# A recommender tower on one core: first-layer products emptied instruction by instruction, with one-sample product matmuls for two of four tiles

## The reference

```python
e = jnp.stack([tbl_0[ids[:, 0]], ..., tbl_26[ids[:, 26]]], axis=1)   # (512, 27, 128)
dot = jnp.einsum('bnd,bmd->bnm', e, e)
z = dot.reshape(512, 27 * 27)[:, idx]        # the 351 pairs i < j
h = jnp.concatenate([z, dense_ctx], axis=1)  # (512, 367)
h = jnp.maximum(h @ W_top1 + b_top1, 0.0)    # 367 -> 512
h = jnp.maximum(h @ W_top2 + b_top2, 0.0)    # 512 -> 256
y = h @ W_top3                               # 256 -> 1
```

## Time and profile before

| | us |
|---|---|
| median of 3 runs (lowest to highest) | 113.99 (113.63 to 115.16) |
| the profiled execution, its own time | 113.77 |
| its span, first to last instruction | 111.9 |
| outside the span | 1.87 |
| mean granted TensorE clock | 0.985 of full speed |

### The profile page before, as it was taken

How to read it: one execution, slowest core, us unless ns; L and a number is a source line. 1 busy time by engine, 2 the same in 40 slices (tenths; PEclk the granted TensorE clock), 3 DMA queues, 4 the chain that set the end, 5 groups by cost and what they waited for, 6 DMA issues and landing times.

```text
span 111.9 us, 2572 instructions
## 1 busy us (share of the span) xinstructions
PE 99.9 (89%) x984; PEld 84.3 (75%) x984; DVE 83.6 (75%) x192; ACT 82.9 (74%) x199; POOL 61.8 (55%) x68
## 2 busy tenths in 40 slices
PE   0956999999999999999997974999999999979882
PEld 0413778878888878888775964999899999969782
DVE  5599699999999999999698079787879438960000
ACT  2568999969969999987906399499999869951230
POOL 0778677777777777777776777677770000000000
PEclk9999999999999999999999997699999999999999
DMA  2989999967944752111221132122220000000000
GB/s 40 330 316 394 342 360 341 391 212 231 270 144 107 236 179 66 48 50 47 70 51 48 47 72 54 47 53 64 57 48 23 9 0 9 0 0 0 6 0 1
DMA packets 6207, 13.33 MB, mean 119 GB/s; under 512 B 2081, under 2 KB 2849, under 8 KB 6066
## 3 DMA queue, kind: packets, MB, share of 16 engines
q1 hardware_dynamic: 3714, 8.62, 23.3%
q0 software_dynamic: 2048, 4.20, 13.6%
q10 hardware_dynamic: 432, 0.34, 1.1%
HBM read 13.15 MB, written 0.00 MB: 118 GB/s over the span
## 4 chain that ended last, share of the span: by engine, by line
PE 67%; DVE 13%; ACT 8%; DMA 6%; issue 2%; SPq 1%; DVEq 0%
PE ps L249 18%; PE ps L250 17%; DVE G L398 12%; PE ps L289 9%; PE ps L307 6%; DMA raw<-in_hot_rows 6%; PE ps L272 5%; ACT G L460 5%; PE ps L261 5%; PE ps L320 3%; PE ps L329 2%; PE ps L338 2%; DVE eT L417 1%; ACT hi L434 1%; SPq L183 1%
## 5 line engine op out<-in xcount | busy, mean ns | idle before, releaser
L224 POOL DMA_INDIRECT E<-in_tbl,ids_sb x64 | 61.5, 962 | 21.7 <-issue 19.2
L386 DVE TENSOR_TENSOR onehot<-idsb,ps 128x1024 fp32r<-128x1024 int16 (+1 forms) x36 | 39.2, 1123 | 2.2 <-DMA idsb<-in_ids_hot 1.2
L398 DVE COPY_PREDICATED G<-mask,ps 27x48 f32<-27x48 int32 (+1 forms) x128 | 27.1, 212 | 11.1 <-ACT G L460 9.0
L460 ACT COPY G<-ps 27x48 f32<-27x48 f32 (+1 forms) x128 | 25.2, 197 | 6.1 <-PE ps L289 4.3
L249 PE MATMUL ps<-onehot,hi 128*128 128x512 f32 x66 | 26.6, 403 | 1.2 <-DVE lo L376 1.2
L250 PE MATMUL ps<-onehot,lo 128*128 128x512 f32 x66 | 25.9, 392 | 0.0
L289 PE MATMUL ps<-eT 128*64 128x54 f32 x512 | 17.7, 234 | 3.1 <-DVE G L398 2.3
L289 PEld LDWEIGHTS ps<-eT 128*64 128x64 f32 x512 | 17.0, 148 | 4.1 <-issue 3.6
L249 PEld LDWEIGHTS ps<-onehot,hi 128*128 128x128 f32 x66 | 12.4, 188 | 5.7 <-DVE lo L376 2.8
L307 PE MATMUL ps<-G,w_sb 128*128 128x128 f32 (+1 forms) x128 | 15.2, 277 | 0.0
L444 ACT ACTIVATE onehot_a<-idsb,num 128x1024 fp32r<-128x1024 int16 (+1 forms) x12 | 13.0, 1080 | 2.6 <-PE ps L250 1.4
(11 more groups left out here) (27 smaller groups left out, 57.7 us busy)
## 6 DMA issues: line engine op xcount, KB each, us to landing
raw<-in_hot_rows SPq DMA_DIRECT2D x10, 512.0 KB, 5.9
idsb<-in_ids_hot SPq DMA_DIRECT2D x5, 256.0 KB, 7.7
E<-in_tbl,ids_sb POOLq DMA_INDIRECT x64, 2.8
w_sb<-in_w SPq DMA_DIRECT2D x1, 1024.0 KB, 7.4
w_sb<-in_w SPq DMA_DIRECT2D x1, 512.0 KB, 7.4
raw<-in_hot_rows ACTq DMA_DIRECT2D x1, 256.0 KB, 3.9
raw<-in_hot_rows SPq DMA_DIRECT2D x1, 256.0 KB, 4.1
idsb<-in_ids_hot SPq DMA_DIRECT2D x1, 128.0 KB, 3.6
```

What stands on the lines that cost most here:

```text
L224: pool.indirect_dma_start(out=E[:, t % ES, slot, :], out_offset=None, in_=tables[f], in_offset=bass.IndirectOffsetOnAxis(ap=ids_sb[:, t * ...
L386: dve.tensor_tensor(onehot[:, u % ONEHOTS, 0:n * B], idsb[:, k0:k0 + n, :].rearrange("p k s -> p (k s)"), ps[:, NUMBERS, c:c + 1].to_broad ...
L398: op = dve.copy_predicated(place(t, w, s, m, n), mask[32 * m:32 * m + F, m:m + 4 * (n - 1) + 1:4].unsqueeze(2).unsqueeze(3) .to_broadcast( ...
L460: op = act.copy(place(t, w, s, m, n), spread(t, w, s, HALF + m, n))
```

## The change

- **Packing.** 24 of 27 slots now stand in 12 blocks of a ring, and three slots (`OWN` to `OWN`+2) are copied again into the five slots that were zeroed (`again`: two VectorE copies within `eT`, 3 x 512 and 2 x 512 elements, at the end of the first stage). So 12 blocks of 30 rows, and three rows left over, hold all pairs; the dense features and the bias go into the free rows. `G` and the first-layer weights have 3 blocks in place of 4: 12 matmuls a tile in place of 16. The four memsets of `eT` are gone.
- **Emptying.** A window is emptied in 16 steps, quadrant by quadrant within each row group. ScalarE signals after every copy, VectorE follows one by one; ScalarE starts a quadrant's next copy when VectorE is done with the one before in that quadrant. After the 16, VectorE does four more predicated copies (32 rows) for the pairs left over.
- **Products.** `EACH = [2, 1, 1, 2]`: tiles 0 and 3 keep two windows of two-sample matmuls. Tiles 1 and 2 have one window each, of 128 matmuls of one sample (32 stationary, 27 moving columns), four column strips in turn; its pieces are twice as long. Eight windows become six.
- **Order.** New lists for the three engines. Tile 3 is transposed in four groups (6, 5, 3, 2). The first part of pair 0 has its ScalarE one-hots last (parts 6, 7). The third layer and the second layer of tile 2 move ahead of the last tile's first layer.
- **Loads.** The second table is loaded ahead of the second ids, half a table moves from SyncE's to ScalarE's queue, dense features come in three small DMAs that wait for the first half of pair 0, as the weights behind them do. GpSimd has no `HOLDS`.

```diff
-GG = [list(range(a, b)) for a, b in [(0, 6), (6, 11), (11, 16)]]
+GG = [[list(range(a, b)) for a, b in zip((0, *ends), ends)] for ends in [[6, 11, 16]] * (T - 1) + [[6, 11, 14, 16]]]
...
-BY_ACT = [(2, 3), (3, 4), (3, 4), (3, 4), (3, 4), (3, 4)]
+BY_ACT = [(6, 7), (3, 4), (3, 4), (3, 4), (3, 4), (3, 4)]
...
-                        what, value = HOLDS.get(t * NG + slot, (None, 0))
-                        if what == "half":
-                            pool.wait_ge(half_done, value)
...
-                for g in range(2 * GB):
-                    at = (g % GB) * 2 * F
-                    for h in range(2):
-                        c = t * P + 64 * h + 2 * (2 * GB * w + g)
-                        mm = pe.matmul(ps[64 * h:64 * h + 64, dots_bank(t, w) + g // GB, at:at + 2 * F],
-                                       eT[:, c:c + 2, :].rearrange("p s f -> p (s f)"), eT[:, c:c + 2, 0:F], start=True, stop=True)
+                for g in range(16):
+                    if EACH[t] == 2:
...
+                    else:
+
+                        for s in range(4):
+                            c = t * P + 64 * (s // 2) + 2 * (16 * w + g) + s % 2
+                            mm = pe.matmul(ps[32 * s:32 * s + 32, window_bank(t, 0) + w, g * F:(g + 1) * F],
+                                           eT[:, c, :], eT[:, c, 0:F], start=True, stop=True)
...
-                for s in range(s0, s0 + ns):
-                    dve.wait_ge(base_out, 4 * (2 * t + w) + s + 1)
-                    for m in range(4):
-                        n = 4 if m == 0 else 3
-                        op = dve.copy_predicated(
...
+                for q in range(s0, s0 + ns):
+                    m, s = divmod(q, 4)
+                    dve.wait_ge(base_step, at + q + 1)
+                    dve.copy_predicated(place(t, w, s, m, ROWS_USED, KT), chosen(t, m, ROWS_USED, m, 4, KT),
+                                        spread(t, w, s, ROWS_USED, m, 4, KT)).then_inc(merge_step, 1)
+                if s0 + ns == 16:
+                    for s in range(4):
+                        dve.wait_ge(merge_step, at + s + 1)
+                        dve.wait_ge(base_step, at + 13 + s)
+                        dve.copy_predicated(place(t, w, s, 0, 32, 2), chosen(t, 0, 32, BLOCKS, 1, 2),
+                                            spread(t, w, s, 32, OWN, 1, 2)).then_inc(dots_out, 1)
...
+                    if m:
+                        act.wait_ge(merge_step, at + q - 3)
+                    act.copy(place(t, w, s, m, ROWS_USED, KT),
+                             spread(t, w, s, ROWS_USED, BLOCKS + m, 4, KT)).then_inc(base_step, 1)
```

More of the change, by code:

```diff
@@ L25 @@
 SPLITS = 4
-GB = 8
-SLOTS = 32
 WARM = 2
+EACH = [2, 1, 1, 2]
+WINDOWS = [(t, w) for t in range(T) for w in range(EACH[t])]
 V = [125000, 1000, 12500, 12500, 1250, 12500, 12500, 12500, 1250, 12500, 12500, 12500, 1000,
@@ L95 @@
[L95 to L100, removed]
+    compare 0 0 4, low 0 0, low 0 1, compare 0 4 2, low 1 0, compare 1 0 2, low 2 0, compare 1 2 1, low 1 1,
@@ L423, in _ @@
             act.dma_start(num[:, :], numbers).then_inc(num_in, 16)
[L424 to L425 removed]
+            for h in range(2):
+                for k in PAIRS[0]:
+                    act.dma_start(raw[:, k, half_of(k, h)], hot_rows[:, k, half_of(k, h)]).then_inc(raw_in[k, h], 16)
             act.dma_start(ident[:, :], eye).then_inc(eye_in, 16)
@@ L506, in _, with pair @@
             act.copy(y[:, :], ps[:, L3, 0:T]).then_inc(y_out, 1)
[L509 to L527 removed]
+def first_layer_rows():
+    take = np.zeros((BLOCKS + 2, 32), np.int32)
+    rows = np.full((BLOCKS, 32), -1)
+    def pair(i, j):
+        a, b = sorted((ORDER[i], ORDER[j]))
+        return b * (b - 1) // 2 + a
+    for k in range(BLOCKS):
+        for i in range(ROWS_USED):
+            if i < OWN:
+                other, second = i % BLOCKS, i >= BLOCKS
+                take[k, i] = second if other <= k else not second
+                if i == k + BLOCKS:
+                    continue
+            else:
+                take[k, i] = i < F
+            slot = i if i < F else AGAIN[i - F]
+            if i == k:
+                take[k, i] = 0
+            rows[k, i] = pair(slot, k if take[k, i] else BLOCKS + k)
+    for n, i in ((0, 30), (0, 31), (1, 31)):
+        take[BLOCKS + n, i] = 1
+        rows[4 * n, i] = pair(AGAIN[i - F], OWN + n)
     assert sorted(rows[rows >= 0]) == list(range(F * (F - 1) // 2))
[L529 removed]
+    return take, rows
 def kernel(**inputs):
@@ L536 @@
     W1 = np.asarray(inputs["W_top1"])
-    rows = first_layer_rows()
+    take, rows = first_layer_rows()
     w1 = np.zeros((4, 32, KT, H1), W1.dtype)
-    for k in range(COLS):
-        used = rows[:, k] >= 0
-        w1[k % 4, used.nonzero()[0], k // 4] = W1[rows[used, k]]
-    w1[2, 0:DENSE, KT - 1] = W1[F * (F - 1) // 2:]
-    w1[2, DENSE, KT - 1] = np.asarray(inputs["b_top1"])
+    for k in range(BLOCKS):
+        used = rows[k] >= 0
+        w1[k % 4, used.nonzero()[0], k // 4] = W1[rows[k, used]]
+    rest = np.zeros((3 * 2 * KT, H1), W1.dtype)
+    rest[0:DENSE] = W1[F * (F - 1) // 2:]
+    rest[DENSE] = np.asarray(inputs["b_top1"])
+    w1[1:, ROWS_USED:] = rest.reshape(3, 2, KT, H1)
+    mask = np.zeros((4, 32, BLOCKS + 2), np.int32)
+    for m in range(4):
+        mask[m] = take.T
     ids = np.asarray(inputs["ids"]).reshape(2, 2, P // 4, T, F).transpose(0, 2, 1, 3, 4)
```

193 lines of the change are left out of this document (90 added, 103 removed).

## The result

The changed kernel takes **109.74 us** (median of 4 runs, 109.06 to 110.25), the kernel before beside it 114.57 (113.63 to 115.67): a ratio of 0.960, 95% interval 0.949 to 0.971. It is faster. I had forecast 112.9 in a range of 109.0 to 116.6. The time lies in the range, but it is that of my first rival (109.3), not of the case I had called likeliest.

What follows compares the result with a forecast made beforehand. First stage bound by TensorE and VectorE together, the second's middle by a mixture, its last tile by emptying. First product 61.8, last emptying 103.6, tail 5.6 to 109.2, plus 1.84 and 1.87: 112.9 us, range 109.0 to 116.6.

Steps and rivals of the forecast that it cites:

- first rival: One-sample products: strips run fully side by side at 0.029 us a matmul, time 109.3 us; chance 0.30.
- the case I had called likeliest: Whole kernel: a tail gain nearly used up by dearer products, 112.9 us, alone 111.5 to 114.3; chance 0.40.
- GpSimd without waits: GpSimd's gathers: removing its waits, all met when it came to them, changes nothing, 0 us.
- First stage: Up to the first product: earlier transposes and two `eT` copies (2.55 us) balance; products start at 61.8 as before, 0.
- Rival 3: First stage: gathers land at 16.5 as before, TensorE stands almost 4 us, clock falls, 116.6 us; chance 0.14.
- Emptying: VectorE's windows: 4.7 us for two-sample tiles, 5.5 for tiles 1 and 2; total 29.8 against 29.2.
- One-sample products: TensorE, tiles 1 and 2: 0.047 us a matmul, four calls 12.0 us against 7.4 before, 4.6 more.
- TensorE's sum: TensorE from 68.9 to tile 3's first product: products, transposes, layers and waits, 22.7 us, to 91.6.
- The tail: After the last emptying: 5.6 us instead of 10.3; of 4.7 gained, 0.9 from packing, the rest from order.

Runs made afterwards that it cites:

- s1_holds: Changed kernel with GpSimd's 27 waits put back, on an undisturbed chip: 120.90 us against 114.19 for the kernel before (1.061).
- r0_same: Changed kernel with nothing altered, on a disturbed chip: 166.04 us against 131.81 for the kernel before (1.257).
- r2_old_tail: Changed kernel with its last steps in the order of the kernel before, on a disturbed chip: 170.92 us, 1.299 of the kernel before.
- r3_two_sample: Changed kernel with two-sample products and two windows in all tiles, on a disturbed chip: 171.99 us, 1.301 of the kernel before.
- u0_no_holds: Kernel before without GpSimd's 27 waits, on a disturbed chip: 173.32 us against 131.50 for the kernel before (1.306).
- e3_twice: Changed kernel with each one-sample product matmul issued twice, on a disturbed chip: 186.06 us, 1.406 of the kernel before.

## Why the prediction came out as it did

By its own steps, on the profiled execution:

- **GpSimd without waits: 0.** For the undisturbed chip this can't be read apart: the pace is 1.25 us a gather as before. Two things were missing. In the order before the waits were met at once, but in the new order they would cost 11.6 us (s1_holds), so the two edits belong together. And on chips of the other kind taking them away costs the kernel before 42 to 44 us. The profile that I had shows nothing of that, and I had no case for it.
- **First stage: 0.** The first product starts at 61.45, mine was 61.8. Behind it two errors met: the transposes began at 14.08 with no wait instead of 14.8 after 2 us of standing, since TensorE's first table matmuls, though they began at 7.90, followed one another at 0.43 us up to 12.2, where those of the kernel before did so at 0.23, which makes some 2 us (the last section has the stretch); and the two `eT` copies took 1.81 us together instead of 2.55 (inside the bounds of 1.3 and 3.8), after which VectorE waited 0.64 for TensorE. Rival 3 did not happen.
- **Emptying.** A two-sample window takes 4.65 against 4.7, and a copy 261 and 230 ns against 253 and 234: right. The one-sample windows are not: 7.5 and 6.2 us against 5.5, since I had ScalarE free for them. It cost nothing here, because TensorE did not stand for them.
- **One-sample products: the term that was mis-sized.** I took 0.047 us a matmul, 12.0 us for four calls; they took 7.95, with the pause of 0.77 in it. The difference is 4.05 us. Tile 3's first product is 4.1 early (87.47 for 91.6), the last predicated copy 4.05 (99.55 for 103.6), and y is ready 3.8 early (105.39 for 109.2), so this one term carries the whole miss: 112.9 - 4.05 = 108.9, measured 109.06. The rest of TensorE's sum holds only in total: 21 transposes took 2.8 us against 2.3, waits 0.7 against 1.2. What went wrong was the reading of the earlier trace rows: records with 128 and with 1 moving column cost the same, but both load all 128 columns, which says nothing of four 32-column strips side by side. I had put that case at 0.30. That rival's 109.3 is near the measured time partly by luck: its price, 0.029, is close to the measured 0.031, but it added 1.0 us of waits for tile 3's gathers, and the trace has none; without them it would have said 108.3. Even its 0.029 was no lower bound, as r0_same's burst price of 0.019 shows.
- The rule of the Trainium skill that I set beside it (TensorE: Matmul & The Clock Gate, "Wait — 56ns, not 53.3ns?"), starts no closer than about 25 ns, doesn't hold here: 128 records in 1.22 us are 9.5 ns apart. By that rule the time would have been 113.7.
- **The tail: 5.6.** To the end of y's copy, as I had summed it, it is 5.84 us (5.68 to its start). But the split into 0.9 by packing and the rest by order was wrong: r2_old_tail gives the order all 4.8 us, 1.6 of them by the clock, for which I had no term.

Summed up: first stage -0.3, from the first product to the last predicated copy +0.15, tail -4.5, makes -4.7 of the profiled 113.8. On its face the gain is the tail alone. The experiments show that the +0.15 is a balance: packing and emptying in turns would cost 5.4 us there (42.98 in r3_two_sample against 37.58 in u0_no_holds, both at full clock and with no gathers beside them), and the mixed products give 6.1 back (36.91 in r0_same).

## What to carry to other kernels

- A wait that is always met at once in one trace may still be doing something: on another chip 42 to 44 us went with it, and in another order of the work it stalled an engine for 11.6. A change that removes such waits is timed on more than one chip.
- Narrow matmuls in separate column strips are cheap in bursts (0.019 us each) and dear in long runs (0.055): in these traces 256 TensorE instructions did not follow one another in under some 3.5 us for long. Spread such calls between slower work, as the changed kernel does.
- Put ready work of TensorE into the wait for the last emptying: it takes work off the tail and keeps the clock up for what follows.

## What was not expected of the hardware

- TensorE's semaphore increments up to 41.5 us late around stretches in which GpSimd issues gathers without a break, on three of the chips that the experiments fell on (a split that ended at 25.87, on which VectorE passed at 63.48), with those of VectorE and ScalarE in time.
- Four strips' matmuls 9.5 ns a record apart in bursts; pauses of up to 2.45 us (e3_twice) a multiple of 256 TensorE instructions apart.
- While GpSimd issues gathers, a one-sample call takes 1.76 to 1.95 us (the changed kernel; 1.76 and 1.79 for the last two of s1_holds), without them 1.22 (r0_same). Only argued: the two go together in all runs, but no run sets them apart on one chip.
- TensorE's first matmuls of the changed kernel follow one another at 0.43 us between 8.5 and 12, twice the later 0.23, while the granted clock reads full there (why is not shown):

```profile
8.40:12.00 3.60, 3.60 (x10) 2.74 (x9) 2.58 (x4) 3.57 (x6) 2.69 (x4) 1.00 1.05 376
```
